# A graph layer's sum over edges: gathered rows as weights, and the root product ahead of it

## The reference, cut to what matters

```python
def _rgcn_conv(x, src, dst, etype, W, root, b):
    x_src = x[src]
    seg = dst * num_rel + etype
    sums = segment_sum(x_src, seg, num_segments=num_nodes * num_rel)
    cnt = segment_sum(ones, seg, num_segments=num_nodes * num_rel)
    mean = (sums / maximum(cnt, 1.0)[:, None]).reshape(num_nodes, num_rel, -1)
    out = einsum('nri,rio->no', mean, W)
    return out + x @ root + b
...
h = relu(_rgcn_conv(xn, src, dst, etype, W1, root1, b1))
gnn = _rgcn_conv(h, src, dst, etype, W2, root2, b2)
x = x + gnn + mix(xn)
```

## Time and profile before

| | us |
|---|---|
| median of 3 runs | 3300.21 (3297.36 to 3302.02) |
| span of the profiled execution | 3506.0 |
| PE busy in it | 3182.0 |
| POOL busy | 1290.4 |
| DVE busy | 1850.6 |
| aggregation, layer 1: first pass to last take | 633.24 to 1141.33 |
| aggregation, layer 2 | 1685.92 to 2190.78 |

### The profile page before, as it was taken

How to read it: one execution, slowest core, us unless ns; L and a number is a source line. 1 busy time by engine, 2 the same in 40 slices (tenths; PEclk the granted TensorE clock), 3 DMA queues, 4 the chain that set the end, 5 groups by cost and what they waited for, 6 DMA issues and landing times.

```text
span 3506.0 us, 63388 instructions
## 1 busy us (share of the span) xinstructions
PE 3182.0 (91%) x19507; PEld 2353.7 (67%) x19508; DVE 1850.6 (53%) x3025; ACT 783.8 (22%) x1113; POOL 1290.4 (37%) x1388
## 2 busy tenths in 40 slices
PE   6999999888888799999888888999987799999999
PEld 5788888666666688888666666677665555555555
DVE  6576666655555433333555555333458755566551
ACT  1211212000000312122000000444521354544550
POOL 2681112566555000001566655100042156434662
PEclk9999999999999999999999999999999899999999
DMA  4334344677776232324677776300033000000003
GB/s 146 107 121 129 116 143 147 202 246 253 236 241 224 79 110 94 117 93 141 213 247 257 244 242 208 125 13 27 13 89 93 19 19 19 1 19 19 19 25 95
DMA packets 101107, 433.91 MB, mean 124 GB/s; under 512 B 19582, under 2 KB 19920, under 8 KB 96757
## 3 DMA queue, kind: packets, MB, share of 16 engines
q0 software_dynamic: 55712, 266.87, 23.6%
q1 hardware_dynamic: 42533, 124.83, 11.3%
q10 hardware_dynamic: 2736, 40.50, 3.3%
HBM read 355.21 MB, written 76.88 MB: 123 GB/s over the span
## 4 chain that ended last, share of the span: by engine, by line
PE 75%; DVE 11%; issue 8%; DVEq 3%; ACT 2%; POOL 1%; DMA 1%; another core or an unknown queue 0%; POOLq 0%; ACTq 0%; SPq 0%
PE PS L1612 25%; PE PS L1747 20%; PE PS L1963 5%; PE PS L1780 3%; PE PS L1621 3%; PE PS L1893 2%; PE PS L1788 2%; DVE NMC L1534 2%; PE PS L1950 2%; PE PS L1825 2%; PE PS L1809 1%; PE PS L1951 1%; PE PS L1799 1%; PE PS L1817 1%; POOL PL L683 1%
## 5 line engine op out<-in xcount | busy, mean ns | idle before, releaser
L1612 PE MATMUL PS<-WHL,XT 128*125 (+1 forms) x3240 | 557.1, 331 | 15.5 <-issue 6.5
L1612 PE MATMUL PS<-WHL,HT 128*125 (+1 forms) x3240 | 535.5, 327 | 3.7 <-issue 2.5
L1612 PEld LDWEIGHTS PS<-WHL,XT 128*125 128x125 f16 (+1 forms) x3240 | 443.9, 139 | 106.0 <-issue 16.1
L1612 PEld LDWEIGHTS PS<-WHL,HT 128*125 (+1 forms) x3240 | 442.9, 137 | 90.3 <-issue 3.8
L1262 DVE SCALAR_TENSOR_TENSOR ROOT<-PS,GS,ROOT x240 | 244.3, 1018 | 339.7 <-remote 136.9
L683 POOL TENSOR_TENSOR PL<-PF 125x500 bf16<-125x500 f32 (+1 forms) x360 | 322.6, 930 | 216.8 <-ACT PF L897 216.0
L1280 DVE SCALAR_TENSOR_TENSOR HOT<-NODE,DSTF,WHLO (+1 forms) x702 | 298.8, 476 | 129.4 <-issue 120.2
L1123 DVE SCALAR_TENSOR_TENSOR MSG<-PS,MSG 125x768 f16<-125x768 f32 x160 | 153.0, 956 | 361.0 <-ACT MSG L722 359.5
L1747 PE MATMUL PS<-GATA,HOT 128*125 128x384 f16 x1440 | 278.9, 353 | 49.6 <-issue 45.1
L722 ACT ACTIVATE MSG<-PS 125x768 f16<-125x768 f32 x160 | 129.7, 811 | 775.4 <-PE PS L1612 770.3
L1747 PE MATMUL PS<-WST,HOT 128*125 128x384 f16 x1404 | 265.4, 346 | 41.4 <-issue 39.2
(11 more groups left out here) (293 smaller groups left out, 4433.9 us busy)
## 6 DMA issues: line engine op xcount, KB each, us to landing
msg_table<-MSG SPq DMA_DIRECT2D x160, 336.0 KB
WST<-in_wg_dram ACTq DMA_DIRECT2D x16, 2304.0 KB, 10.0
WST<-in_wf_dram SPq DMA_DIRECT2D x7, 1536.0 KB, 6.7
KROW<-key_rows POOLq DMA_DIRECT2D x54, 192.0 KB, 3.8
msg_table<-MSG SPq DMA_DIRECT2D x160, 39.0 KB
WST<-in_wm_dram SPq DMA_DIRECT2D x5, 1152.0 KB, 5.1
GATA<-msg_table,SKEY POOLq DMA_INDIRECT x216
WST<-msg_table,SKEY POOLq DMA_INDIRECT x216
```

Of the source, the lines that this page charges most:

```text
L1612: ins = pe.matmul(PS[0:ROWS, b0 + h, 0:HALF], X[:, xp, k, bass.ts(t, ROWS)], panel_part(slot, wp, k, h), start=k == 0 and xp + wp == 0, st ...
```

## The change

The roles in the aggregation are exchanged. A group has four tiles (81 groups) and three sets of slots (12 slots, none in `WST`). The gathered rows are the weights now: a chunk of 128 features of 128 edges is loaded, and the one-hots of 32 nodes move past it, high and low part together (64 columns) past the high rows, the high part alone (32 columns) past the low rows. A tile has 12 weight loads and 12 matmuls, a group 48 of each. The sums stand feature by node, in `ACC` (128 by 6 by 1282), and a group's window begins at its first destination; a loop over windows stays for groups that reach further than 32 nodes. PE reads one register a group (`PASSES`), DVE two (`LIM`, `PASSES`). DVE makes the one-hots in two steps, comparison and product, for four tiles at once, and adds the group before with two instructions of 192 elements.

The root panel is turned as well: 18 pieces of 18 matmuls (weights from the panel, 500 or 250 columns of nodes moving), all of them ahead of the first group. ACT fills `ACC` with the bias first. At layer 2's start nothing is transposed: ACT and DVE split `ACC` directly. After layer 2 PE turns `ACC` back by 60 transposes, ACT copies the rows to `ROW`, SP stores them, and PE's mix waits for the last copy.

```diff
-AT = 3
+AT = 4
 AG = TILES // AT
-GSETS = 6
...
+GSETS = 3
+GSLOTS = GSETS * AT
+WIN = 32
...
+ROOT_FIRST = 18
...
+PIECES = [(m, c) for c in range(len(CHUNKS)) for m in range(KT)]
+ROOT_BANK = (6, 3)
...
-                    if t == STAGED:
-                        if L == 0:
-                            edge_weights(0)
-                        g.wait_ge(S["w_lo"], (REL + 1) * (L + 1) + 1)
+                    if t == GSLOTS and L == 0:
+                        edge_weights(0)
+                    if t % AT == 0 and L * AG + grp >= GSETS:
+                        g.wait_ge(S["group_read"], L * AG + grp - GSETS + 1)
                         g.sem_inc(S["pool_tick"], 1)
-                    if t % AT == 0:
-                        if grp >= GSETS:
-                            g.wait_ge(S["group_read"], AG * L + grp - GSETS + 2)
-                            g.sem_inc(S["pool_tick"], 1)
-                        elif L == 1:
-                            g.wait_ge(S["group_used"], AG + 1)
-                            g.sem_inc(S["pool_tick"], 1)
...
+                act.activation(HT[:, 0, :, t * ROWS:(t + 1) * ROWS], ACC[:, :, t * ROWS:(t + 1) * ROWS], ACT.Relu, scale=HSC[:, HSCALE]).then_inc(S["h_hi"], 1)
...
+            for t in range(RT):
+                act.wait_ge(S["gnn_t"], t + 1)
+                if t >= 4:
+                    act.wait_ge(S[f"gnn_out{t % 4}"], ROW_IN * (t // 4))
+                act.activation(halves(ROW[:, t % 4, :]), rowps(4 + 2 * (t % 2)), ACT.Copy).then_inc(S["gnn_made"], 1)
...
+                    v.tensor_scalar(HTMP[:], ACC[:, :, t * ROWS:(t + 1) * ROWS], 0.0, HSC[:, HSCALE], ALU.max, ALU.mult)
+                    v.drain()
                     v.wait_ge(S["h_hi"], t + 1)
-                    v.scalar_tensor_tensor(xtview(HT, 1, t), tview(4), HSC[:, HSCALE], xtview(HT, 0, t), ALU.mult, ALU.subtract).then_inc(S["h_free"], 1)
...
+                def take_root(r):
+
+                    m, c = PIECES[r]
+                    c0, n = CHUNKS[c]
                     v.drain()
+                    v.wait_ge(S["root_done"], len(PIECES) * L + r + 1)
+                    v.scalar_tensor_tensor(ACC[:, m, c0:c0 + n], PS[:, ROOT_BANK[r % 2], 0:n], OUTINV[:], ACC[:, m, c0:c0 + n], ALU.mult, ALU.add).then_inc(S["root_out"], 1)
...
+                def make_hots(grp, p):
+
+                    tiles = slice(grp * AT, (grp + 1) * AT)
+                    v.tensor_tensor(SAME[:], NODE[:, bass.ds(p * WIN, WIN)].unsqueeze(1).broadcast_to([128, AT, WIN]),
+                                    DREL[:, tiles].unsqueeze(2).broadcast_to([128, AT, WIN]), ALU.is_equal)
                     v.drain()
+                    v.tensor_tensor(HOT[:, grp % GSETS], SAME[:].unsqueeze(2).broadcast_to([128, AT, 2, WIN]),
+                                    WHLO[:, tiles, :].unsqueeze(3).broadcast_to([128, AT, 2, WIN]), ALU.mult).then_inc(S["hot_made"], 1)
+
+                def take_pass():
+
+                    v.drain()
+                    v.wait_ge(S["pass_done"], v.snap(cnt, min_val=0, max_val=1 << 20) + (L + 1))
+                    w0 = v.snap(was, min_val=0, max_val=N - 1)
+                    bank = v.snap(was_bank, min_val=0, max_val=GSETS - 1)
+                    columns = ACC[:, :, bass.ds(w0, WIN)]
+                    sums = PS[:, bass.ds(bank, 1), 0:KT * 2 * WIN].rearrange("p a (k w c) -> p (a k) w c", w=2, c=WIN)
+                    for w in range(2):
+                        ins = v.scalar_tensor_tensor(columns, sums[:, :, w, :], GS[:, 2:3], columns, ALU.mult, ALU.add)
+                        if w == 0:
+                            v.drain()
+                    ins.then_inc(S["pass_out"], 1)
...
+                for grp in range(AG):
+                    first = v.value_load(LIM[0:1, grp:grp + 1], min_val=0, max_val=N - 1)
+                    n_passes = v.value_load(PASSES[0:1, grp:grp + 1], min_val=1, max_val=WINDOWS)
+                    v.reg_mov(ready, 1)
+                    with v.Fori(0, n_passes) as p:
+                        v.wait_ge(S["pass_done"], v.snap(ready, min_val=1, max_val=1 << 20))
+                        make_hots(grp, p)
+                        take_pass()
+                        v.reg_mov(was, first + p * WIN)
+                        v.reg_mov(was_bank, grp % GSETS)
+                        v.reg_add(cnt, cnt, 1)
+                        v.reg_mov(ready, v.snap(cnt, min_val=0, max_val=1 << 20) + (L + 1))
...
+                def root_piece(r):
+
+                    m, c = PIECES[r]
+                    c0, n = CHUNKS[c]
+                    if len(PIECES) * L + r >= 2:
+                        pe.wait_ge(S["root_out"], len(PIECES) * L + r - 1)
+                    for k in range(KT):
+                        for wp, xp in ((0, 0), (0, 1), (1, 0)):
+                            ins = pe.matmul(PS[:, ROOT_BANK[r % 2], 0:n], WHL[:, (REL + L) % 2, wp, k * D + m * 128:k * D + (m + 1) * 128], X[:, xp, k, c0:c0 + n],
+                                            start=k == 0 and wp + xp == 0, stop=k == KT - 1 and wp == 1)
+                    ins.then_inc(S["root_done"], 1)
+
+                for r in range(ROOT_FIRST):
+                    if L == 0 and r < TAIL:
+                        find_counts(REL * RT + r - COUNTED * RT)
+                    if r == 1:
+                        pe.wait_ge(S["pair_out"], ROW_SUMS * (L + 1) + 2)
+                    root_piece(r)
+                    weights_top(r)
...
+                pe.matmul(PS[:, GSETS - 1, 0:KT * 2 * WIN], ZERO[:, 0:128], ZERO[:, 0:KT * 2 * WIN], start=True, stop=True).then_inc(S["pass_done"], 1)
+                r = ROOT_FIRST
+                for grp in range(AG):
+                    n_passes = pe.value_load(PASSES[0:1, grp:grp + 1], min_val=1, max_val=WINDOWS)
+                    pe.reg_mov(taken, 1)
+                    with pe.Fori(0, n_passes):
+                        pe.wait_ge(S["pass_out"], pe.snap(taken, min_val=1, max_val=1 << 20))
+                        pe.wait_ge(S["hot_made"], pe.snap(cnt, min_val=0, max_val=1 << 20) + 1)
+                        for k in range(AT):
+                            t = grp * AT + k
+                            pe.wait_ge(S[f"gat_in{t % GSLOTS}"], 16 * (TILES // GSLOTS * L + t // GSLOTS + 1))
+                            rows = gat_slot(t % GSLOTS)
+                            for c in range(KT):
+                                o = PS[:, grp % GSETS, c * 2 * WIN:(c + 1) * 2 * WIN]
+                                pe.matmul(o, rows[:, c * 128:(c + 1) * 128], HOT[:, grp % GSETS, k].rearrange("p w c -> p (w c)"), start=k + c == 0, stop=False)
+                                ins = pe.matmul(o[:, 0:WIN], rows[:, D + c * 128:D + (c + 1) * 128], HOT[:, grp % GSETS, k, 0, :], start=False, stop=k == AT - 1 and c == KT - 1)
+                        ins.then_inc(S["pass_done"], 1)
+                        pe.reg_add(cnt, cnt, 1)
+                        pe.reg_mov(taken, pe.snap(cnt, min_val=0, max_val=1 << 20) + (L + 2))
+                    pe.matmul(PS[:, 7, 320:322], ZERO[:, 0:128], ZERO[:, 0:2], start=True, stop=True).then_inc(S["group_read"], 1)
...
             pe.wait_ge(S["rows_done"], 2)
+            for t in range(RT):
+                if t >= 2:
+                    pe.wait_ge(S["gnn_made"], t - 1)
+                for k in range(KT):
+                    ins = pe.transpose(PS[0:ROWS, 4 + 2 * (t % 2) + k // 3, (k % 3) * 128:(k % 3 + 1) * 128], ACC[:, k, t * ROWS:(t + 1) * ROWS], IDF[:])
+                ins.then_inc(S["gnn_t"], 1)
+            pe.wait_ge(S["gnn_made"], RT)
```

More of the change, by code:

```diff
@@ L1288, in _ @@
-                v.wait_ge(S["root_made"], RT * (L + 1))
-                first = 0
-                for i, t in ROOT_AT[L]:
-                    passes(first, i + 1)
-                    root_row(t, 6)
-                    first = i + 1
-                passes(first, TURNS)
-                for n_ in range(LAG_PASS):
-                    take_pass(v.snap(cnt, min_val=0, max_val=1 << 20) + n_, was[2 - n_])
-                v.sem_inc(S["group_used"], 1)
+                    v.tensor_tensor(HOT[:, grp % GSETS], SAME[:].unsqueeze(2).broadcast_to([128, AT, 2, WIN]),
+                                    WHLO[:, tiles, :].unsqueeze(3).broadcast_to([128, AT, 2, WIN]), ALU.mult).then_inc(S["hot_made"], 1)
@@ L1686, in _ @@
                     pe.wait_ge(S["bounds_made"], 1)
-                    for n_ in range(2):
-                        ins = pe.transpose(PS[0:1, 5, n_ * AG:(n_ + 1) * AG], GB[:, 2 + n_:3 + n_], IDF[0:AG, 0:AG])
-                    ins.then_inc(S["bounds_t"], 1)
+                    pe.matmul(PS[:, 5, 0:2 * AG], ONEK[:], DIAG[:].rearrange("p a g -> p (a g)"), start=True, stop=True).then_inc(S["bounds_t"], 1)
                 else:
-                    transpose_h(0)
                     pe.wait_ge(S["w_lo"], REL + 2)
@@ L1711, in weights_top @@
                         top_broadcast((REL + 1) * (L + 1))
-                for t in range(ROOT_AT[L][0][1]):
```

(19 more changed lines are left out.)

236 lines of the change are left out of this document (89 added, 147 removed).

## The result

The changed kernel takes 3377.73 us (median), the kernel before 3301.11 in the same runs: a ratio of 1.0233, 95% interval 1.0217 to 1.0249, so 2.3% slower. One of its four runs took 5745.36 us, at a granted clock of 1.0 and for a reason that no trace here shows; the ratio leaves it out. The time lies in the predicted range (3222 to 3405) and on the side that was thought likelier, but outside the forecast's own 3294 to 3345: the forecast of 3312 us was far too small a step.

A forecast was written before the change was run, and what follows sets the result against it. The prediction took POOL's gathers to bound the changed aggregations, with PE's floor before nearly as high. 3506.0 - 79.6 - 73.8 - 10 + 12 = 3354.6 us profiled, less 42, gave 3312 us, range 3222 to 3405.

The forecast's parts named there:

- the side that was thought likelier: Whole kernel: slower than before, chance 0.49, against 0.36 for faster and 0.15 for the same.
- 1.28 was taken: Aggregation: POOL needs 1.28 us a tile unhindered, so 312 gathers take 399.4 us.
- The panel: Root work ahead of each aggregation: 57.1 us of matmuls, plus 7.9 in layer 1 and 5.7 in layer 2.
- two slower rivals: Aggregation: PE stays at the lower clock (3409 us, chance 0.19), or half the groups need two windows (3410, 0.03).
- s: The part of the profiled execution's 206 us over the median that lies outside the two aggregations, taken as 42.
- I take a quarter of that, 42: A quarter of 166 us idle elsewhere: 42, making an undisturbed aggregation 424 us, 5% above POOL's floor.
- the traced execution's 3354.6: Whole kernel: the changed kernel's predicted time in a profiled run, 3354.6 us, before 42 us were taken off.
- Layer 2's start was to gain 10: Start of layer 2: ten sets of six transposes and the DVE waits behind them leave, about 10 us less.
- The end was to cost 12: End of layer 2: PE's 60 transposes back, the first copy and DVE's last take, 12 us more.
- The faster one: Aggregation: POOL is quicker outside the profile, or the kernel before wastes more; 3219 to 3293 us, chance 0.36.
- The lower-clock rival: Aggregation: PE falls to the lower clock and stays, 113 ns a pair, 5.7 us a group; 3409 us, chance 0.19.
- the windows: Aggregation: half of the groups need two windows, PE taking 121 passes of 3.8, 460 us; 3410 us, chance 0.03.

The follow-up runs named there:

- e5_before_half: The kernel before the change without the second half of layer 2's edges (162 tiles): 3099.73 us.
- e8_extents: The changed kernel with a group's number of windows found by one comparison and one sum instead of 40 dependent instructions: 3368.03 us.
- e9_lookahead: The changed kernel with three rows of the hidden state split ahead at layer 2's start instead of one: 3366.36 us.
- e7_stores_first: The changed kernel with SP's ten stores after layer 2 moved above its load of the mix's second weights: 3364.38 us.
- e6_after_half: The changed kernel without the second half of layer 2's edges (160 tiles left out): 3176.65 us.
- e12_no_low: The changed kernel without the 24 matmuls of a group that multiply the low rows: 3374.86 us.
- e4_half_rows: The changed kernel with the same gathers each fetching rows of 768 values instead of 1536, half of the bytes: 3372.25 us.

## Why the prediction was right, and why it was too small

**Right: the bound.** POOL at 1.26 us a tile sets the aggregation (1.28 was taken), PE idles half of it, the panel ahead is serial and POOL stands still beside it (43.65 us). The panel was put at 65.0 us from the first root piece to the panel's end in layer 1 (67.8 measured) and 62.8 in layer 2 (57.6). From the first piece to the last take the sum had 476.9 and 474.7 us; measured are 472.1 and 461.8. That the time lies in the range at all is in part luck: what held the range open above 3345 were the two slower rivals (3409 and 3410), and neither came.

**Wrong: s.** The step "I take a quarter of that, 42" was the largest miss. It put an aggregation 5% above its floor and had no row for the quarter. Half of an aggregation costs 200.6 us (e5_before_half) and one lasts 406.3, so s is about 6: the kernel before loses almost nothing against POOL's floor, and nothing of that sort was left to gain. The profile's stalls were gains only on paper. From the traced execution's 3354.6 some 6 us were to be taken off and not 42: 36 of the 65 us between forecast and result.

**Wrong: three hand-overs, of which one was not priced at all.** The start of the kernel had no term, and cost 16.2 us: 8.19 of PE waiting for the 40-step count of windows (9.7 by e8_extents) and 4.05 for edge counting that now stands ahead of the first piece (`find_counts` in the diff). The 4.05 are read from the trace alone: no run takes them out by themselves. Layer 2's start was to gain 10 and gained 0.5: the transposes went, but PE's waits for the split stayed (9.4 us, 8.2 before) and some of its rows ran at a lower clock (e9_lookahead gives 11.4). The end was to cost 12 and cost 24.4; the step counted PE's transposes and the first copy, but not the queue that the stores are in: SP has five loads ahead of them (13.3 by e7_stores_first). These three make 38 us; the panels and aggregations ended 18 us sooner than their sum, and 3 us lie between the span and the median: with the 36 above, 59. The 6 us that are left are s itself: the hand-overs are measured against stages of the first profiled execution, which hold it.

**The rivals.** The faster one falls: s is not 100, and the runs pay POOL's 0.30 us in full (1.257 us a tile in e6_after_half). The lower-clock rival had the clock right: it is 0.50, the lower level of 1.2 GHz, through the stage, where PE works on one or two tiles at a time between waits of up to 2.8 us. The rule of the Trainium skill that speaks against the change ("TensorE: Matmul & The Clock Gate", section "HAM oscillation — how this bites in real kernels") said that PE would keep falling back to it, and the trace agrees. The rival's price was wrong. A pair costs 40 ns at half clock, not 113: the row that priced it moves 136 columns, a pair of the change 48 on average, and either way that is 0.83 ns a column. And e12_no_low shows that PE's work is worth nothing there. Of the windows nothing was seen: DVE made 162 comparisons in the two layers, one for each of 81 groups.

## What to carry to other kernels

A floor that two engines share is not lowered by relieving one of them: before rebuilding a stage, leave out half of its work and see what a tile costs in undisturbed runs. Work that runs free beside a bound engine becomes serial when it is moved ahead of it. When a data layout changes, price the hand-overs at either end, and for each store or copy what stands ahead of it in its queue.

## What the runs showed of the hardware that was not expected

An indirect gather of 128 rows holds POOL for 0.95 us, with 0.30 us to the next, whether a row has 1536 bytes (e4_half_rows) or 3072; at 3072 that is 304 GB/s with the DMA engines 0.88 busy. Matmuls of 64 and 32 columns with 128 columns of 16-bit weights loaded for each start every 27 ns at full clock and every 40 ns at half clock on average. One profiled execution can be slower than every timed run, by 206 us here, with nearly all of the stalls in two stages; the sign was there to be read, in a span far above the median. What stalled that execution is left open: the profile puts 50.9 us of PE's idle time ahead of the passes of layer 1 down to "issue", where e5_before_half has 5.2.
